# Last layer's input built already transposed: x transposed from HBM, HF and spread means added on GpSimd, instead of transposes on TensorE in three of four groups

## The reference

```
h = max(layernorm(x), 0)
x = x + L0(h)      # two graph layers, then LSTMs over windows of 1, 2, 3, 4 nodes
h = max(layernorm(x), 0)
x = x + L1(h)

def L0(h):
    h = relu(adj @ (h @ Wg0 + bg0))
    h = relu(adj @ (h @ Wg1 + bg1))
    for p in (1, 2, 3, 4):      # window length
        last = LSTM_p(windows of p nodes of h)       # hidden state after p steps
        h[:, last node of each window] = last
    return h

def L1(h):                     # three products with W[k], then by parts of adj
    v = h @ W[k]    (k = 0, 1, 2)
    return diag(adj) v[0] + triu(adj, 1) v[1] + tril(adj, -1) v[2] + bias
```

## Time and profile before

| | |
|---|---|
| median of 3 runs | 401.47 us (401.32 to 401.8) |
| span of the profiled execution | 399.1 us |
| what lies around the span (median less span) | 2.4 us |
| TensorE busy | 393.3 us, 99% |
| VectorE busy | 346.5 us, 87% |
| ScalarE busy | 287.4 us, 72% |
| GpSimd busy | 44.0 us, 11% |
| TensorE clock granted | 1.00 of full in every slice |

### The profile page before, as it was taken

How to read it: one execution, slowest core, us unless ns; L and a number is a source line. 1 busy time by engine, 2 the same in 40 slices (tenths; PEclk the granted TensorE clock), 3 DMA queues, 4 the chain that set the end, 5 groups by cost and what they waited for, 6 DMA issues and landing times.

```text
span 399.1 us, 6598 instructions
## 1 busy us (share of the span) xinstructions
PE 393.3 (99%) x2394; PEld 345.3 (87%) x2394; DVE 346.5 (87%) x886; ACT 287.4 (72%) x579; POOL 44.0 (11%) x44
## 2 busy tenths in 40 slices
PE   8999999999999999999999999999999999999997
PEld 7787889998987789899877879899797788989886
DVE  6569999998998998887998898988898979787897
ACT  4668777875897777777689676777589677767554
POOL 4910200100300003000110000300020000000250
PEclk9999999999999999999999999999999999999999
DMA  7830000000000000000000000000000000000003
GB/s 205 315 140 2 0 0 2 2 0 2 0 1 2 26 28 0 28 2 1 2 16 10 28 0 29 0 28 1 2 2 26 0 28 26 2 26 3 0 0 133
DMA packets 5503, 11.18 MB, mean 28 GB/s; under 512 B 1120, under 2 KB 2528, under 8 KB 4960
## 3 DMA queue, kind: packets, MB, share of 16 engines
q1 hardware_dynamic: 5472, 10.77, 7.5%
HBM read 6.57 MB, written 4.19 MB: 27 GB/s over the span
## 4 chain that ended last, share of the span: by engine, by line
PE 79%; DVE 14%; ACT 4%; issue 1%; DMA 1%; POOL 0%; SPq 0%; DVEq 0%; ACTq 0%
PE PS L549 11%; PE PS L540 11%; PE PS L541 10%; PE PS L572 6%; PE PS L569 6%; PE PS L568 6%; PE PS L615 5%; PE PS L490 4%; PE PS L480 4%; PE PS L472 4%; PE PS L457 3%; PE PS L607 3%; PE PS L608 3%; PE PS L609 3%; ACT GT L869 2%; PE PS L582 1%
## 5 line engine op out<-in xcount | busy, mean ns | idle before, releaser
L869 ACT ACTIVATE GT<-PS,BG 128x256 f32<-128x256 f32 (+2 forms) x312 | 157.9, 563 | 17.5 <-PE PS L572 12.8
L540 PE MATMUL PS<-HH,WIH 128*128 128x256 f32 (+2 forms) x312 | 107.2, 344 | 0.1
L541 PE MATMUL PS<-HH,WIL 128*128 128x256 f32 (+2 forms) x312 | 102.7, 330 | 0.0
L549 PE MATMUL PS<-HL,WIH 128*128 128x256 f32 (+2 forms) x294 | 97.3, 331 | 0.6
L884 ACT ACTIVATE TC<-CS 128x512 f32<-128x512 f32 (+2 forms) x88 | 44.9, 510 | 43.6 <-DVE CS L1014 32.5
L387 POOL TENSOR_TENSOR RS<-VE,NHALF 128x4 f32<-128x4 f32 (+2 forms) x18 | 29.9, 1661 | 344.5 <-DVE VE L950 263.9
L540 PEld LDWEIGHTS PS<-HH,WIH 128*128 128x128 f32 x312 | 58.8, 188 | 9.3 <-DVE HH L1052 4.3
L541 PEld LDWEIGHTS PS<-HH,WIL 128*128 128x128 f32 x312 | 58.9, 189 | 3.9 <-issue 1.2
L549 PEld LDWEIGHTS PS<-HL,WIH 128*128 128x128 f32 x294 | 55.5, 189 | 6.6 <-DVE HL L1060 2.4
L572 PE MATMUL PS<-SL,WHH 128*128 128x256 f32 (+2 forms) x192 | 60.1, 313 | 0.2
L568 PE MATMUL PS<-SH,WHH 128*128 128x256 f32 (+2 forms) x192 | 59.9, 312 | 0.0
(11 more groups left out here) (95 smaller groups left out, 655.5 us busy)
## 6 DMA issues: line engine op xcount, KB each, us to landing
out_tbd<-X SPq DMA_DIRECT2D x15, 256.0 KB, 2.0
X<-x_tbd SPq DMA_DIRECT2D x3, 1024.0 KB, 12.9
WI<-wih_t SPq DMA_DIRECT2D x1, 1024.0 KB, 5.2
X<-x_tbd SPq DMA_DIRECT2D x3, 256.0 KB, 3.7
WH<-whh_t SPq DMA_DIRECT2D x1, 768.0 KB, 6.6
X<-x_tbd SPq DMA_DIRECT2D x2, 128.0 KB, 2.4
WL<-w_l SPq DMA_DIRECT2D x1, 192.0 KB, 6.4
WG<-wg SPq DMA_DIRECT2D x2, 64.0 KB, 2.8
```

Source lines behind the costliest of these rows:

```text
L540: pe.matmul(dst, WIH[:, p - 1, cols], x_high, start=True, stop=False)
L541: pe.matmul(dst, WIL[:, p - 1, cols], x_high, start=False, stop=False)
L549: mm = pe.matmul(dst, WIH[:, p - 1, cols], x_low, start=False, stop=(j == 0))
L869: act.activation(GT[:, s, q, 0:n], bank(s, q)[:, 0:n], ACT.Tanh if q == C else ACT.Sigmoid, bias=BG[:, 4 * (p - 1) + q:4 * (p - 1) + q + 1 ...
```

## The change

Until the change TensorE transposes the centred x of every quad. After it, for groups 0 to 2, H3 holds the features on the partitions from the start. SP loads a group's x from a second, host-transposed input x_dbt straight into H3 (1 MB per group, in the order of HF). After the last LSTM units GpSimd adds HF to it, quad by quad. SP writes MINUS2 of a stream to a DRAM scratch (pieces of 8 bytes), reads it back on all 128 partitions into U, which is free then, and GpSimd adds that too. ScalarE's ReLU and VectorE's low part read H3 instead of PSUM. Waits change with it: ScalarE's HTH waits for `centred`, VectorE waits for `xt_summed` before it writes HF again, SP holds the spreads ahead of the stores. `centre_up` and CENTRE disappear in groups 0 to 2. In the plans the TURN pieces go, quad 2 is read by ScalarE at (6, 0) and quad 3 at (10, 0), and some VALUE and SUM pieces stand one or two units from where they were. The batches of HTH and HTL now lie in pairs, so that a value matmul loads its weights with a stride of two elements. The last group is as it was.

```diff
-START = {(1, 1): (Piece(TURN, 0, 1, None),), (1, 3): (Piece(SUM, -1, 0, None),),
...
+TURN_AT = {(1, 1): 0, (4, 1): 1, (6, 0): 2, (10, 0): 3}
...
+START_LATE = {4: ((OWN, 0),), 5: ((LOW, 2), (SHIFT, 0)), 6: ((SHIFT, 1), (SHIFT, 2)), 9: ((LOW, 3), (SHIFT, 3))}
...
+        def turned_x(q):
+
+            return H3[:, quad(q), :].rearrange("p b t -> p (b t)")
+
+        def turned_h(q):
+
+            s, half = divmod(q, HBANKS)
+            return HF[:, s, half * HALF:(half + 1) * HALF, :, :].rearrange("p c t e -> p (c t e)")
+
+        def means(q):
+
+            s, half = divmod(q, HBANKS)
+            return U[:, s, half * PACK * T:(half + 1) * PACK * T]
+
+        def of_batch(h, g, b):
+
+            if g == GROUPS - 1:
+                return h[:, b * T:(b + 1) * T]
+            return h.rearrange("p (c t e) -> p c t e", c=HALF, e=2)[:, b // 2, :, b % 2]
...
+            def load_turned(g):
+
+                if g > 0:
+                    sp.wait_ge(turn_low, QUADS * g)
+                sp.dma_start(H3[:, :, :].rearrange("p b t -> p (b t)"), x_dbt[:, g, :]).then_inc(xt_in, 16)
+
+            def spread_means(g, s):
+
+                n = STREAMS * g + s
+                sp.wait_ge(var2, 2 * n + 1)
+                sp.dma_start(MEANS[g, s, :].rearrange("(c t e) -> t c e", c=HB // 2, e=2),
+                             MINUS2[:, s * HB:(s + 1) * HB].rearrange("t (c e) -> t c e", e=2)).then_inc(means_out, 16)
+                sp.wait_ge(means_out, 16 * (n + 1))
+                sp.wait_ge(z_mm, 2 * HBANKS * (g + 1) + HBANKS * (s + 1))
+                sp.dma_start(U[:, s, :], MEANS[g, s, :].rearrange("(a n) -> a n", a=1).broadcast_to([128, HB * T])
+                             ).then_inc(means_in, 16)
...
-            for i in range(GROUPS):
-                store(i)
+            load_turned(0)
+            for i in range(GROUPS - 1):
+                for s in range(STREAMS):
+                    spread_means(i, s)
+                if i > 0:
+                    store(i - 1, (LAST,))
+                store(i, range(LAST))
+                if i < GROUPS - 2:
+                    load_turned(i + 1)
+            store(GROUPS - 2, (LAST,))
+            store(GROUPS - 1, range(QUADS))
...
+                pool.wait_ge(xt_in, 16 * (i + 1))
+                for s in range(STREAMS):
+                    pool.wait_ge(lstm_step, STEPS * i + STEPS_BEFORE[LAST_OF[s] + 1])
+                    for q in range(HBANKS * s, HBANKS * (s + 1)):
+                        pool.tensor_tensor(turned_x(q), turned_x(q), turned_h(q), ALU.add).then_inc(xt_summed, 1)
                 for s in range(STREAMS):
                     if i > 0:
 
                         pool.wait_ge(value_sb, G * (i - 1) + HB * (s + 1))
                     rstd(VE2, var2, 2 * STREAMS * i + 2 * s + 2, RS2, rs2, HB * s, HB * s + HB)
+                    pool.wait_ge(xt_summed, QUADS * i + HBANKS * (s + 1))
+                    pool.wait_ge(means_in, 16 * (STREAMS * i + s + 1))
+                    for q in range(HBANKS * s, HBANKS * (s + 1)):
+                        pool.tensor_tensor(turned_x(q), turned_x(q), means(q), ALU.add).then_inc(centred, 1)
...
-                act.wait_ge(turn_mm, QUADS * g + q + 1)
+                if g == GROUPS - 1:
+                    act.wait_ge(turn_mm, q + 1)
+                else:
+                    act.wait_ge(centred, QUADS * g + q + 1)
                 act.activation(HTH[:, q % 2, :], ps, ACT.Relu).then_inc(turn_high, 1)
...
-                for q in range(ON_SCALAR):
-                    centre_up(i, q)
...
+                if i > 0 and last_unit(k, s) is None:
+
+                    dve.wait_ge(xt_summed, QUADS * (i - 1) + HBANKS * (s + 1))
```

More of the change, by code:

```diff
@@ L109 @@
-START_LATE = {4: ((OWN, 0),), 5: ((CENTRE, 2), (SHIFT, 0)), 6: ((SHIFT, 1), (SHIFT, 2))}
+START_MID = {0: ((OWN, -1),), 4: ((LOW, 1),), 5: ((ADD, 0),), 8: ((OWN, 1),), 9: ((ADD, 1),), 12: ((OWN, 2),)}
+START_LATE = {4: ((OWN, 0),), 5: ((LOW, 2), (SHIFT, 0)), 6: ((SHIFT, 1), (SHIFT, 2)), 9: ((LOW, 3), (SHIFT, 3))}
 STEADY = Plan(
[L111 to L114, removed]
@@ L117 @@
-LATE = Plan(at=START, f_after={**START_F, 16: (TURN, 3), 17: (SUM, 2)}, quads=LAST,
-            between=START_BETWEEN, mid=START_MID, late={**START_LATE, 9: ((CENTRE, 3), (SHIFT, 3))})
+    at={**START, (13, 3): (Piece(VALUE, 12, 0, (FORGET, 12)),), (15, 1): (Piece(VALUE, 13, 0, (VALUE, 12)),),
+        (16, 3): (Piece(VALUE, 14, 1, (SUM, 2)),), (17, 3): (Piece(VALUE, 15, 0, (FORGET, 16)),)},
+    f_after={**START_F, 16: (VALUE, 13), 17: (VALUE, 14), 18: (VALUE, 15)},
+    quads=QUADS, between=START_BETWEEN, mid=START_MID, late=START_LATE)
@@ L119 @@
+LATE = Plan(at=START, f_after={**START_F, 17: (SUM, 2)}, quads=LAST,
+            between=START_BETWEEN, mid=START_MID, late=START_LATE)
 PLANS = (None,) + (GROUPS - 2) * (STEADY,) + (LATE,)
@@ L223, in program @@
         PS = ctx.enter_context(nc.psum_tensor("PS", [128, 8, 512], F32))
+        MEANS = nc.dram_tensor("means", (GROUPS - 1, STREAMS, HB * T), F32, kind="Internal").ap()
         x_first = sem("x_first")
@@ L275, in program @@
         pool_shifted = sem("pool_shifted")
-        turned_up = sem("turned_up")
         centred = sem("centred")
+        xt_in = sem("xt_in")
+        xt_summed = sem("xt_summed")
+        means_out = sem("means_out")
+        means_in = sem("means_in")
         turn_mm = sem("turn_mm")
@@ L355, in _, with store @@
                 sp.dma_start(X[:, g * G:(g + 1) * G, :], x_tbd[:, g * G:(g + 1) * G, :]).then_inc(x_rest, 16)
-            def store(i):
-                for q in range(QUADS):
+            def load_turned(g):
[11 more added lines that the diff above has]
+                             ).then_inc(means_in, 16)
+            def store(i, quads):
+                for q in quads:
                     pieces = END_PIECES if i == GROUPS - 1 and q == LAST else ((0, PACK),)
@@ L604, in last_value @@
                 dst = ps[:, 0:PARTS * D]
-                high, low = (h[:, q % 2, b * T:b * T + T] for h in (HTH, HTL))
+                high, low = (of_batch(h[:, q % 2, :], g, b) for h in (HTH, HTL))
                 w_high, w_low = (w[:, :, :].rearrange("p k e -> p (k e)") for w in (WLH, WLL))
@@ L814, in copy_value @@
                                scale=RS2[:, n:n + 1]).then_inc(value_sb, 1)
-            def centre_up(g, q):
-                if q == 0:
-                    act.wait_ge(var2, 2 * STREAMS * g + 1)
-                for b in range(q * PACK, (q + 1) * PACK):
-                    done = act.activation(H3[:, b, :], X[:, g * G + b, :], ACT.Relu, bias=MINUS2[:, b:b + 1])
-                done.then_inc(turned_up, 1)
             def last_copy(piece, g):
-                if piece.what == TURN:
-                    turn_up(g, piece.n, bank(piece.s, F))
-                elif piece.what == VALUE:
+                if piece.what == VALUE:
                     copy_value(g, piece.n, bank(piece.s, F))
@@ L865, in unit @@
                 for m, q in enumerate(gates):
+                    if plan and j == 0 and (k, m) in TURN_AT:
+                        turn_up(i - 1, TURN_AT[k, m], turned_x(TURN_AT[k, m]))
                     for piece in plan.at.get((k, m), ()) if plan and j == 0 else ():
```

50 lines of the change are left out of this document (19 added, 31 removed).

## The result

The changed kernel takes 415.92 us (median of 4 runs, 414.56 to 416.7) against 401.41 before it: ratio 1.0358, interval 1.0339 to 1.0378. It is 14.5 us slower. The profiled execution has a span of 412.8 us, 13.7 more than in the earlier trace rows.

The account below looks back on a forecast made before the run. The prediction took TensorE, busy 99% of the span, as the bound, with VectorE barely behind. A's 4.4 plus B's 4.3 minus 4.0 for the turns gave +4.7 on 401.5: 406.2 us, range 402.5 to 411.

Parts of the forecast that it names:

- A: Between groups: GpSimd's adds of HF for quads 0 and 1 hold VectorE, 4.4 us late over three passages.
- B: Units 0 to 4: GpSimd's adds of the means hold VectorE, 4.3 us late, each group's first turn swallowed in it.
- the nine turns behind: TensorE turns after each group's first: removed transposes gain 9 x 0.44 = 4.0 us.
- VectorE waits for the whole add: VectorE instructions with two SBUF inputs wait out a GpSimd add beside them, up to its full 1.27 us.
- the first rival: Beside the adds only GpSimd waits; A and B are 0, all twelve turns gain: 396.2 us, chance 0.25.
- The turns on TensorE: Twelve quads in groups 0 to 2 lose four transposes each, worth 0.44 us apiece, 5.3 at most.
- Plan shifts: Value and sum pieces moved one or two units find TensorE full: 0, at most 0.24 us either way.
- the stride: Value matmuls' two-element-stride loads of HTH and HTL: extra load hidden, taken as 0; 1.4 us if not.
- ScalarE's 24 activations less: 24 activations of 388 ns leave ScalarE where it waits for TensorE anyway: no gain.
- the wait of HTH: ScalarE's first HTH per group waits for centred: 2 us to spare in group 0, more in groups 1 and 2.
- third rival: The spread of the means comes late and delays ScalarE's HTH: 422 us at most, chance 0.05.
- The slack takes B: VectorE waits, but its gaps and the removed centring absorb the means; A stays: 400.6 us, chance 0.13.

Follow-up runs that it names:

- e1: Changed kernel with all 24 GpSimd adds (HF and means) cut to 8 of 512 columns: 401.62 us, ratio 1.0002.
- e7: Kernel before, plus two unneeded GpSimd adds of 128x512 per group in groups 0 to 2: 405.09 us, ratio 1.0095.
- e10: Kernel before, plus two GpSimd memsets of 128x1024 per group in groups 0 to 2: 400.96 us, ratio 0.9989.
- e3: Changed kernel with only the adds of the means cut to 8 columns, adds of HF full: 405.62 us, ratio 1.0103.
- e4: Changed kernel without the spread's DMAs through DRAM and the wait on them, all adds full size: 409.97 us, ratio 1.0217.
- e9: Kernel before, with one transpose in place of four at each quad's turn in groups 0 to 2: 399.84 us, ratio 0.9966.
- e5: Changed kernel with value 7, sum 1 and the own part of quad 1 back at their old places: 414.91 us, ratio 1.0324.
- e11: Changed kernel with the new way only for quads 2 and 3, adds of HF after both streams: 404.55 us, ratio 1.0077.
- e12: As e11, but the two adds of the means each wait for VectorE's bias adds of earlier quads: 403.49 us, ratio 1.0054.
- e6: Changed kernel with value matmuls loading neighbouring columns in place of every second one: 414.19 us, ratio 1.0321.
- e2: Changed kernel with only the adds of HF cut to 8 columns, adds of the means full: 410.41 us, ratio 1.0233.
- e8: Changed kernel with the adds of HF started only when both streams are through unit 21: 409.64 us, ratio 1.02.

## Why the prediction was right in its sign and wrong in its size

The prediction was 406.2, in a range up to 411; 415.92 came. Its mechanism holds, and two of its three terms have the wrong size. By the lateness, each term counted as the prediction counts it:

| term | predicted | changed kernel | e1, no adds |
|---|---|---|---|
| A, adds of HF between groups | 2.2 + 1.1 + 1.1 = 4.4 | 2.00 + 1.56 + 1.20 = 4.76 | 0 + 0.52 + 0.18 = 0.70 |
| B, adds of the means, units 0 to 4, first turn of each group in it | 2.3 + 1.0 + 1.0 = 4.3 | 2.93 + 2.92 + 2.25 = 8.1 | -0.2 |
| the nine turns behind, and all the rest | -4.0 | +0.3 | -0.6 |

- **VectorE waits for the whole add: shown.** By e7 (adds without the change, +3.8), e10 (memsets, none of it) and e1 (without the adds, +0.2). With it the first rival, "VectorE never waits", falls. The Trainium skill, page SBUF — State Buffer, section Who interferes with whom, has a VectorE instruction with two SBUF inputs contend with a GpSimd instruction that reads SBUF, and not with one that only writes it, the other engine blocked in full; the 1.40 and 1.49 of L1042 and L1052 agree, and so does the memset of e10.
- **A: right, in place and in size.** Less what e1 shows without adds, the three passages cost 2.00 + 1.04 + 1.02 = 4.06 against the 4.4 of the forecast, and 3.8 to 4.0 by medians where the adds of HF stand alone (e7, e3 less e1).
- **B: the step that failed first.** "Of 2 x 1.27 = 2.5 I take half, 1.3" per pair, less 0.8 and 0.8 of slack: 4.3 forecast, 8.1 measured. Three things were wrong in it. The trip was 7.2 us and not the "5 to 6 us" from a 256 KB store and load, so the first pair came 1.3 later behind MINUS2 than the sum has it (it stands at 109.61 and not at 106.3; 2.0 of these 3.3 are A's lateness). The second pair was held for 2.1 of its 2.5 and not for half: 0.98 at CAST, 1.10 at L1039, and then came the tanh and the value copy behind it on ScalarE, of which the sum took only VectorE's part. And in group 2 the slack of 1.6 wasn't there: the loss was 2.9 as in group 1. e4 puts a number on the place: 4.6 to 6 us go when the same adds come some 5 to 6 us earlier. B alone, on a kernel without A, is 8.8 by the medians, some 2.2 of that by the clock in the profiled execution.
- **The turns on TensorE: the other step that failed.** "All twelve are worth 12 x 0.44 = 5.3 us at most", and "9 x 0.44 = 4.0 of gain is left": nothing of it was left, for e1, without any add, is no faster than the kernel before. The 0.44 do come off where TensorE has less to do: in group 1 of e1 -0.50 between units 1 and 2, -0.33 between 7 and 8, -0.52 between 18 and 19. But the same group loses 0.41 at units 3 and 4, 0.31 at unit 6, 0.31 at unit 7 and, net, 0.39 from unit 8 to 11, and the 0.52 of its end in the passage to group 2. e9, with the plan as before, keeps 1.6 of 4.0. The prediction reads TensorE's 77.66 of 77.9 us in the earlier trace rows so that an instruction taken out "is a gain, if its inputs also come earlier", and never put a price on that condition. It is the condition that failed.
- **Plan shifts, "0, and at most the idle that the earlier trace rows shows in a group's steps, 0.24, either way": right for value 7 and sum 1, wrong for quad 2.** By e5 the first two cost nothing by unit 11, for all the 1.02 of idle time that they make. But ScalarE now reads quad 2 at (6, 0), ahead of a value copy. Timeline, ScalarE, of the kernel before, then of e1:

```profile
125.45 0.56 ACT L812 ACTIVATE WH<-PS,RS 128x384 f32<-128x384 f32 x1
...
125.55 0.62 ACT L853 ACTIVATE HTH<-H 128x512 fp32r<-128x512 f32 x1
126.07 0.55 ACT L866 ACTIVATE WH<-PS,RS 128x384 f32<-128x384 f32 x1
```

  The copy comes 0.62 later, and the value matmuls behind it need the bank that it empties: TensorE, 0.11 late at unit 6, is 0.40 late at the second of them (126.97 against 126.57). This is the 0.31 at unit 7, which e1 has in each of the three groups. e11 and e12 read quad 2 at (8, 0) and have 0.03 or less there.
- **What cost nothing, as predicted:** the stride; ScalarE's 24 activations less; the wait of HTH, which had 1.7 us to spare in group 1 even with the longer trip. The third rival's way (ScalarE idle at HTH) did not happen, but its cause, a trip of over 7 us, did, and cost through VectorE.
- **"The slack takes B"** did not happen: no slack took anything before unit 4, as was argued against it.

The scatter of the runs is large: 414.56 to 416.7 here, 411.79 to 415.6 in e5, 412.22 to 416.24 in e6, against 0.5 for the kernel before. Much of it is TensorE's clock. The profiled executions of e2, e5, e6 and e8 have stretches at a clock of 0.50 after the stall at units 3 and 4; one such stretch of 3.4 us lowers the mean granted clock of a run by 0.004. The fastest run of the changed kernel (414.56, the profiled one) has a mean clock of 1.00, the other three, 1.1 to 2.1 us slower, have 0.995 and 0.996. e6 has 1.00 at 412.22 and 412.71, and 0.991 and 0.992 at 415.66 and 416.24. So some 1.4 of the 14.5 us are the clock's by these four runs, and 13.1 remain at full clock.

What stays open: the 0.31 at unit 6 of group 1. In e1 TensorE waits there for the low part of quad 1 (HTL), in e9 it loses 0.27 at the same place, and no run takes it apart. Also 1.05 us that the changed kernel loses more than e1 from unit 4 of group 3 on, and the scatter at full clock: e5 has 411.79 and 414.89, both with a mean clock of 1.00.

## What to carry to other kernels

Idle time on GpSimd isn't free time: in this kernel each of its instructions that reads SBUF had to be priced at its full duration on VectorE, unless VectorE then stood idle (e12) or had a PSUM input or bn_stats (e8). Ask what stands behind the held instruction on the other queues. A transfer that nobody waits for still decides where the work behind it falls. On an engine that is 99% busy, as TensorE here, count removed work as a gain only after checking that the inputs of what follows are early by as much.

## What the runs showed of the hardware

- Tiny instructions are held like large ones. Timeline of the changed kernel, VectorE, in the passages to group 1 and to group 3:

```profile
102.20 0.17 DVE L990 TENSOR_SCALAR MINUS<-LN 128x8 f32<-128x8 f32 x1
...
305.52 1.30 DVE L986 TENSOR_TENSOR LN<-ST 128x8 f32<-128x8 f32 x1
...
306.82 1.25 DVE L990 TENSOR_SCALAR MINUS<-LN 128x8 f32<-128x8 f32 x1
```

  Operations of eight columns go from 0.17 to 1.25 and 1.30. One of them has a single tile as input (L990), as has the CAST at 116.31 (1.41, against the 0.43 that it takes undisturbed), so it isn't only instructions with two SBUF inputs, as the prediction drew it from the earlier trace rows (though it named the cast among its signs). The same section of the Trainium skill, page SBUF — State Buffer, says that casts and tensor_scalar can contend too; these two rows agree.
- The DMA of 4 KB in pieces of 8 bytes took 3.4 us, longer than the 2.0 of a 256 KB store.
- TensorE's granted clock stood at 0.50, 1.2 GHz, for about 3.4 us each time it fell in the middle of these kernels, soon after idle times of 1.7 to 2.3 us, in e2 (rows above), e5, e6 and e8. It stayed at 1.00 after 1.73 and 3.11 us in the profiled execution of the changed kernel, and after 1.75 in e5 and e8. In groups 2 and 3 the units right behind such a stretch came 1.4 to 1.6 us later than without it; in group 1 it was 1.3 to 1.4, about half of it made up by the end of the group. It does not happen each time.
